# Attention of a graph transformer: where the last unit of a pair is multiplied, and the order of two vector operations in each unit

## The chip, the cores and the metric

One NeuronCore of a Trainium2 chip runs the whole program. The metric is the device time of one execution in microseconds. Engines: PE is TensorE (matmuls; PEld is its weight load), ACT ScalarE, DVE VectorE, POOL GpSimd; SP issues DMAs. Each engine works its own queue in order, and semaphores tie the queues together.

## The reference

Four blocks of a graph network on 3125 nodes with 128 features and 100000 edges, each with a layer norm and a residual. The change touches only the fourth, a transformer of four layers:

```python
for l in range(4):
    Q, K, V = h @ WQ[l] + bQ[l], h @ WK[l] + bK[l], h @ WV[l] + bV[l]
    scores = jnp.sum(Q[dst] * K[src], axis=-1) * scale
    e = jnp.exp(scores - segment_max(scores, dst)[dst])
    attn = e / segment_sum(e, dst)[dst]
    messages = segment_sum(attn[:, None] * V[src], dst)
    h = _layernorm(h + messages @ WO[l] + bO[l], ln_g[l], ln_b[l])
```

## The kernel before

The kernel computes the attention densely. The 3125 nodes are 25 tiles (NT) of 125 (T). A block of 125 destinations gets a row of scores against all 3125 sources; a bias from DRAM, made once from the edge counts, removes the pairs without an edge and gives repeated edges their weight. Blocks go in pairs: pairs 0 to 11 have two blocks ("halves"), pair 12 (LAST_PAIR) has one. `after_pairs` runs pair 0, then a loop over two pairs at a time (their buffers are told apart by e = 1 and 0), then pairs 11 and 12. There are three layers in an outer loop and a fourth written out (its tiles are named l_last_...).

A row of scores is made in 7 chunks (NC), four of 500 and three of 375 columns, so a pair has 14 (PAIR_CHUNKS; g counts them, 0 to 13; g = 14, 15, 16 are chunks 0, 1, 2 of the pair after that). Per chunk:

- **scores** (PE, L1755): three matmuls (high and low parts of q and k), into one of three PSUM banks (S_BANKS). A bank has to have been read: three chunks back, or two back where a new pair begins.
- **maximum** (DVE, L1852): one instruction reads the bank, adds the bias, writes the row buffer and keeps the maximum; a short read of the accumulator follows. After the last chunk of a block, L1858 makes the negated maximum that the exponential needs.
- **exponential** (ACT, L1811): in place on the row buffer. Its schedule, in the step of ACT, is not touched.

The finished rows are turned and multiplied by the values in 13 units (UNITS) of two tiles, the last of one tile. Per unit u:

- **turn** (PE, L1771): four transposes (two in unit 12) into one of three PSUM banks (T_BANKS).
- the **copy** (ACT, L1822): writes the high part of the turned tiles to SBUF (`operand(..., 0)`, tile awcol).
- **low_part** (DVE, L1862): the turned tiles minus their high part.
- **weigh** (PE, L1783): two matmuls per tile, with the high and low parts of the values as weights, which accumulate a pair's sum in `sum_ps[e]`. It waits for low_part of its unit.
- **finish**: ACT (L1817, in unit 1 of the next pair) and DVE (L1870 and L1875, in unit 2) read the sum of the pair before.

The order of the work is written out by hand, in the step function of each engine. On PE a unit of a pair is: scores of chunks ahead, turn(u), weigh(u - 1); after unit 12, weigh(12) stands right behind weigh(11). `ahead` (L1675) says which chunks belong to a unit: AHEAD is 3, so unit 0 takes g = 3 and 4, unit u from 1 on takes g = u + 4, and unit 12 takes g = 16. On DVE a unit is: the maxima of the same chunks, then low_part(u), then in unit 2 the finish. `first` makes the first 17 chunks of a layer before pair 0. Pair 12 makes no scores, and pair 11 has only g = 3 to 6 to make.

Of the kernel before, what the change touches and what calls it, by code (L numbers as in the profile page):

```python
# [25 lines left out]
NC = (NT + 3) // 4  # L26
# [1414 lines left out]
def transformer(nc, G):  # L1441
# [5 lines left out]
    UNITS, PAIR_CHUNKS, HALF, AHEAD = (NT + 1) // 2, 2 * NC, 256, 3  # L1447
    LAST_PAIR = NT // 2
# [3 lines left out]
    with ExitStack() as ctx:  # L1452
# [101 lines left out]
        def layer(l, last, tag):  # L1554
            with ExitStack() as held:
# [20 lines left out]
                with ExitStack() as pre:  # L1576
# [4 lines left out]
                    with nc.Block() as block:  # L1581
                        @block.sync
                        def _(sp):
                            for p in range(2):
                                sp.dma_start(bias[p][:, :], G["bias_dram"][p, :, :]).then_inc(bias_in[p], 16)
# [51 lines left out]
                with ExitStack() as loop:  # L1637
# [21 lines left out]
                    def after_pairs(eng, step):  # L1659

                        step(0, 0)
                        with eng.Fori(0, (LAST_PAIR - 2) // 2) as i:
                            step(2 * i + 1, 1)
                            step(2 * i + 2, 0)
                        step(LAST_PAIR - 1, 1)
                        step(LAST_PAIR, 0)

                    single = lambda P: isinstance(P, int) and P == LAST_PAIR
                    units = lambda P: range(NC if single(P) else UNITS)
# [4 lines left out]

                    def ahead(P, e, u, act_on):  # L1675

                        for k in ((0, 1) if u == 0 else (u + 1,)):
                            g = k + AHEAD
                            to, f = (P + 1, 1 - e) if g < PAIR_CHUNKS else (P + 2, e)
                            half, c = divmod(g % PAIR_CHUNKS, NC)  # L1680
                            if exists(to, half):
                                act_on(to, f, half, c)

                    def first(act_on, chunks=PAIR_CHUNKS + AHEAD):
                        for g in range(chunks):
                            P, (half, c) = g // PAIR_CHUNKS, divmod(g % PAIR_CHUNKS, NC)
                            act_on(P, P, half, c)

                    def operand(P, e, u, low):

                        n, wide = len(tiles(P, u)), T if single(P) else 2 * T
                        buffer = wcol[slot(P, e, u)][:, :, :]
                        if single(P):
                            buffer = buffer.rearrange("p t (a d) -> p (t a) d", a=2)
                        at = low * buffer.shape[2] // 2
                        return buffer[:, 0:n, at:at + wide]

                    def turned(P, e, u):
                        n, wide = len(tiles(P, u)), T if single(P) else 2 * T
                        return turned_ps[slot(P, e, u)][:, 0:n * wide].rearrange("p (t d) -> p t d", d=wide)  # L1700

                    with nc.Block() as block:
# [37 lines left out]
                        @block.tensor  # L1740
                        def _(pe):
                            pe.sem_inc(turned_ready, 2 * UNITS)

                            def scores(P, e, half, c):
                                a, z = CHUNKS[c]
                                b, g = 2 * P + half, NC * half + c
                                if c == 0:
                                    pe.wait_ge(q_staged, 2 * b + 2)

                                back = 3 if g >= S_BANKS else PAIR_CHUNKS + g - max(k for k in range(PAIR_CHUNKS) if k % S_BANKS == g)  # L1750
                                pe.wait_ge(scores_read, b * NC + (c - back + 1 + NC))
                                z += (z - a) % 2
                                terms = ((q_high, k_low), (q_low, k_high), (q_high, k_high))
                                for n, (left, right) in enumerate(terms):
                                    last = pe.matmul(s_ps[g % S_BANKS][:, 0:z - a], left[half][:, :], right[:, a:z],  # L1755
                                                     start=(n == 0), stop=(n == len(terms) - 1))
                                last.then_inc(scores_ready, 1)

                            def turn(P, e, u):
                                ts = tiles(P, u)  # L1760
                                halves = 1 if single(P) else 2
                                pe.wait_ge(exp_done, (2 * P + halves - 1) * NC + (chunk_of(ts[-1]) + 1))
                                if u >= T_BANKS:
                                    pe.wait_ge(low_made, P * UNITS + (u - T_BANKS + 1 + UNITS))
                                else:
                                    before = UNITS + u - T_BANKS if e else max(k for k in range(UNITS) if slot(0, 1, k) == u)
                                    pe.wait_ge(low_made, P * UNITS + (before + 1))
                                for j, t in enumerate(ts):
                                    for half in range(halves):
                                        at = (halves * j + half) * T  # L1770
                                        last = pe.transpose(turned_ps[slot(P, e, u)][:, at:at + T], row[2 * e + half][:, t * T:(t + 1) * T], ident[0:T, 0:T])  # L1771
                                last.then_inc(turned_ready, 1)

                            def weigh(P, e, u):
                                if u == 0:
                                    pe.wait_ge(sum_read, P + 1)
                                pe.wait_ge(low_made, P * UNITS + (u + 1 + UNITS))
                                wide = HALF if single(P) else 2 * HALF
                                buffer = wcol[slot(P, e, u)][:, :, :].rearrange("p t d -> p (t d)")
                                for j, t in enumerate(tiles(P, u)):  # L1780
                                    terms = ((vals_high, wide), (vals_low, HALF))
                                    for n, (left, n_cols) in enumerate(terms if t == 0 else terms[::-1]):
                                        last = pe.matmul(sum_ps[e][:, 0:n_cols], left[:, t, :], buffer[:, j * wide:j * wide + n_cols],  # L1783
                                                         start=(t == 0 and n == 0), stop=(t == NT - 1 and n == 1))
                                if u == units(P)[-1]:
                                    last.then_inc(sum_ready, 1)

                            def step(P, e):

                                for u in units(P):  # L1790
                                    if not single(P):
                                        ahead(P, e, u, scores)
                                    turn(P, e, u)
                                    if u:
                                        weigh(P, e, u - 1)
                                weigh(P, e, units(P)[-1])
                            first(scores)
                            after_pairs(pe, step)

                        @block.scalar  # L1800
                        def _(act):
# [36 lines left out]
                        def _(dve):  # L1838
# [21 lines left out]
                            def low_part(P, e, u):  # L1860
                                dve.wait_ge(high_copied, P * UNITS + (u + 1))
                                dve.tensor_tensor(operand(P, e, u, 1), turned(P, e, u), operand(P, e, u, 0).bitcast(FP32), ALU.subtract  # L1862
                                                  ).then_inc(low_made, 1)
# [12 lines left out]

                            def step(P, e):
                                for u in units(P):
                                    if not single(P):
                                        ahead(P, e, u, maximum)  # L1880
                                    low_part(P, e, u)
                                    if u == 2 and not (isinstance(P, int) and P == 0):
                                        finish(P - 1, 1 - e)
                            first(maximum)
                            after_pairs(dve, step)
                            finish(LAST_PAIR, 0)

# [74 lines left out]
        with nc.Fori(0, LAYERS - 1) as l:  # L1962
            layer(l, False, "l3")
        layer(LAYERS - 1, True, "l3_last")

        with ExitStack() as final:
# [90 lines left out]
```

## Time and profile before

| | us |
|---|---|
| median of 3 runs | 3178.64 (3176.86 to 3182.97) |
| the profiled execution, its own time | 3186.86 |
| its span | 3185.1 |
| PE busy | 2573.7 (81%) |
| DVE busy | 2451.7 (77%) |
| ACT busy | 1956.1 (61%) |
| POOL busy | 221.1 (7%) |

The attention loops lie between about 1725 us and 3150 us of the span. Matmuls are pipelined: a matmul's reported duration (0.39 us for 500 columns) is longer than the distance to the next one's start (0.23 us), so distances between starts show PE's real pace, and an idle time shown before a matmul is shorter than the time lost.

### The profile page before, as it was taken

The page shows a single profiled execution, that of the slowest core. Times are in us where ns is not written, and L with a number is a line of the kernel's source. Part 1 is how long each engine was busy: PE and PEld are TensorE (multiplying, and loading weights), DVE is VectorE, ACT ScalarE, POOL GpSimd, SP SyncE. Part 2 cuts the span into 40 slices and gives each one's busy share as a digit, 9 for nine tenths or more (in the row PEclk, how much of TensorE's full clock was granted, in tenths as well). Part 3 has the DMA queues.
Part 4 walks back from the last instruction along what each step waited for, and adds up shares of the span by engine and source line. Part 5 has one row for each costly group of instructions (what it writes and reads, how often), then busy time and mean ns, then how long its engine had stood idle before and what let it go on. Part 6 is the DMA issues. An engine that isn't in the chain of part 4 may idle for free. (4 is left out here: it accounts for less than half of the span.)

```text
span 3185.1 us, 60275 instructions
## 1 busy us (share of the span) xinstructions
PE 2573.7 (81%) x19197; PEld 2090.7 (66%) x19197; DVE 2451.7 (77%) x5292; ACT 1956.1 (61%) x3958; POOL 221.1 (7%) x487
## 2 busy tenths in 40 slices
PE   0788888756378887888846999789996999969997
PEld 0555555446366666666635888668885888858886
DVE  7999999735489998999976777667775777667776
ACT  1666666512278887788844666556674666646664
POOL 3000000000000000000001111011110111011110
PEclk9999999878689998889978999899998999979998
DMA  1233233462342326332303333033321433123331
GB/s 41 85 115 126 89 124 127 164 219 84 96 128 104 120 102 179 116 109 103 122 5 112 142 123 138 27 140 124 141 103 45 143 133 128 63 103 124 138 136 46
DMA packets 87373, 355.45 MB, mean 112 GB/s; under 512 B 47453, under 2 KB 59541, under 8 KB 59796
## 3 DMA queue, kind: packets, MB, share of 16 engines
q1 hardware_dynamic: 87149, 352.59, 31.9%
q8 instruction: 125, 2.05, 0.3%
q14 instruction: 99, 0.81, 0.1%
HBM read 285.86 MB, written 65.67 MB: 110 GB/s over the span
## 5 line engine op out<-in xcount | busy, mean ns | idle before, releaser
L1822 ACT ACTIVATE awcol<-l_aturned 125x500 fp32r<-125x500 f32 (+2 forms) x489 | 279.2, 572 | 290.8 <-PE l_aturned L1771 288.8
L1365 PE MATMUL gturned<-ident,grow 125*125 125x125 f32 x2500 | 410.3, 306 | 29.2 <-ACT grow L1303 29.2
L1862 DVE TENSOR_TENSOR awcol<-l_aturned,awcol 125x500 fp32r<-125x500 f32 (+2 forms) x489 | 321.2, 657 | 109.9 <-ACT awcol L1822 102.1
L1365 PEld LDWEIGHTS gturned<-ident,grow 125*125 125x125 f32 x2500 | 332.8, 204 | 107.5 <-issue 73.0
L1272 DVE SCALAR_TENSOR_TENSOR grow<-line,a_dst 125x3125 f32<-125x3125 f32 x100 | 347.6, 3476 | 40.3 <-DMA line<-lines_dram 24.7
L1783 PE MATMUL l_asum<-awcol,vals_high 125*128 125x512 f32 (+1 forms) x975 | 360.1, 390 | 19.0 <-DVE awcol L1862 19.0
L1303 ACT ACTIVATE grow<-grow,neg 125x3125 f32<-125x3125 f32 x100 | 290.4, 2904 | 122.6 <-DVE neg L1284 122.6
L1281 DVE CUSTOM_DVE_ANT_0 grow<-grow,bias 125x3125 f32<-125x3125 f32 x100 | 341.7, 3417 | 24.4 <-DMA bias<-bias_dram 10.2
L1343 PE MATMUL gparts<-gwcol,h_mem 125*32 125x125 f32 x5000 | 245.1, 290 | 113.9 <-ACT gwcol L1316 113.9
L1783 PE MATMUL l_asum<-awcol,vals_low 125*128 125x256 f32 x975 | 305.0, 322 | 13.5 <-DVE awcol L1862 12.9
L1316 ACT ACTIVATE gwcol<-gturned 125x1000 f32<-125x1000 f32 x300 | 282.0, 1002 | 19.2 <-PE gturned L1365 19.1
L1343 PEld LDWEIGHTS gparts<-gwcol,h_mem 125*32 125x32 f32 x5000 | 133.3, 114 | 170.7 <-ACT gwcol L1316 73.1
L449 DVE TENSOR_SCALAR hot_key<-iota_key,fixed 128x325 bf16<-128x325 f16 x1000 | 242.2, 315 | 0.0
L503 PE MATMUL win<-hot_key,hot_place 128*125 128x325 bf16 x750 | 140.0, 308 | 122.5 <-DVE hot_key L449 103.7
L1755 PE MATMUL l_scores<-k_low,l_q_high 128*125 128x500 f32 (+1 forms) x525 | 201.3, 383 | 27.5 <-POOL l_q_low L1730 19.3
L564 ACT ACTIVATE blk<-win 125x325 f32<-125x325 f32 x250 | 96.9, 445 | 197.6 <-PE win L514 197.6
L503 PEld LDWEIGHTS win<-hot_key,hot_place 128*125 128x125 bf16 x750 | 90.8, 138 | 189.8 <-DVE hot_key L449 86.4
L1783 PEld LDWEIGHTS l_asum<-awcol,vals_high 125*128 125x128 f32 x975 | 184.7, 189 | 43.2 <-DVE awcol L1862 18.8
L1852 DVE CUSTOM_DVE_ANT_0 arow<-l_scores,abias 125x500 f32<-125x500 f32 (+1 forms) x252 | 154.8, 622 | 74.5 <-PE l_scores L1755 56.8
L1783 PEld LDWEIGHTS l_asum<-awcol,vals_low 125*128 125x128 f32 x975 | 184.8, 190 | 31.8 <-DVE awcol L1862 30.0
L1755 PE MATMUL l_scores<-k_high,l_q_low 128*125 128x500 f32 (+1 forms) x525 | 194.0, 369 | 0.0
L1755 PE MATMUL l_scores<-k_high,l_q_high 128*125 128x500 f32 (+1 forms) x525 | 193.9, 369 | 0.0
(346 smaller groups left out, 5769.8 us busy)
## 6 DMA issues: line engine op xcount, KB each, us to landing
abias<-bias_dram SPq DMA_DIRECT2D x100, 1562.5 KB, 6.5
bias<-bias_dram SPq DMA_DIRECT2D x50, 1562.5 KB, 6.6
bias_dram<-lnrow SPq DMA_DIRECT2D x25, 1562.5 KB, 5.2
counts_dram<-pair SPq DMA_DIRECT2D x13, 1562.5 KB, 6.5
pair<-counts_dram SPq DMA_DIRECT2D x13, 1562.5 KB, 16.4
line<-lines_dram SPq DMA_DIRECT2D x8, 1367.2 KB
fixed<-kp SPq DMA_DIRECT2D x250, 4.0 KB, 1.7
agg<-counts_dram SPq DMA_DIRECT2D x2, 1367.2 KB
```

The costliest lines, as they stand in the source:

```text
L449: last = dve.tensor_scalar(hot_key[p][:, i, keys], G["iota_key"][:, keys], fixed[r][:, k, i, 0:1], base, ALU.subtract, ALU.is_equal)
L503: pe.matmul(win[p][:, k, 0:KEYS[k]], hot_place[p][:, k, i, 0:T], hot_key[p][:, i, keys], start=(i == 0), stop=False)
L1272: dve.scalar_tensor_tensor(out=row[n % RING][:, :], in0=line[g][:, 0, :], scalar=a_dst[:, b, k:k + 1], in1=line[g][:, 1, :], op0=ALU.add, ...
L1281: dve.tensor_tensor_reduce(out=here, in0=here, in1=bias[i % 2][0:T, :], scale=1.0, scalar=-3.0e38, op0=ALU.add, op1=ALU.max, accum_out=top ...
L1303: act.activation(row[n % RING][:, :], row[n % RING][:, :], ACT.Exp, bias=neg[:, b, k:k + 1], accum_out=den[:, b, k:k + 1]).then_inc(exp_do ...
L1316: act.activation(wcol[q % RING][:, :].rearrange("p (g n) -> p g n", g=2), bank[q % RING][:, :, 0:C4], ACT.Copy).then_inc(col_copied, 1)
L1343: last = pe.matmul(part_ps[CH * j:CH * (j + 1), at:at + T], vals[:, t, k, :], wcol[q % RING][:, (t - t0) * T:(t - t0 + 1) * T], start=(t < ...
L1365: last = pe.transpose(bank[q % RING][:, j // 4, j % 4 * T:(j % 4 + 1) * T], row[n % RING][:, t * T:(t + 1) * T], ident[0:T, 0:T])
L1755: last = pe.matmul(s_ps[g % S_BANKS][:, 0:z - a], left[half][:, :], right[:, a:z], start=(n == 0), stop=(n == len(terms) - 1))
L1783: last = pe.matmul(sum_ps[e][:, 0:n_cols], left[:, t, :], buffer[:, j * wide:j * wide + n_cols], start=(t == 0 and n == 0), stop=(t == NT ...
L1822: act.activation(operand(P, e, u, 0), turned(P, e, u), ACT.Copy).then_inc(high_copied, 1)
L1862: dve.tensor_tensor(operand(P, e, u, 1), turned(P, e, u), operand(P, e, u, 0).bitcast(FP32), ALU.subtract).then_inc(low_made, 1)
```

## The change

Three edits in the steps of the attention loop.

1. `ahead` moves every chunk from g = 4 to g = 15 one unit later: unit u takes g = u + 3, and unit 12 takes g = 15 and 16. Before, unit 0 had two chunks; now unit 12 has. `ahead` serves PE (scores) and DVE (maximum) alike.
2. On PE, weigh of a pair's unit 12 no longer follows weigh(11) but stands in unit 0 of the next pair, behind turn(0). After pair 12, its own last unit is weighed at the end, as before.
3. On DVE, low_part(u) comes ahead of the maxima of the unit.

```diff
                     def ahead(P, e, u, act_on):
-                        for k in ((0, 1) if u == 0 else (u + 1,)):
+                        for k in ((u, u + 1) if u == UNITS - 1 else (u,)):
                             g = k + AHEAD
...
                                     turn(P, e, u)
                                     if u:
                                         weigh(P, e, u - 1)
-                                weigh(P, e, units(P)[-1])
+                                    elif not (isinstance(P, int) and P == 0):
+                                        weigh(P - 1, 1 - e, UNITS - 1)
                             first(scores)
                             after_pairs(pe, step)
+                            weigh(LAST_PAIR, 0, NC - 1)
...
                                 for u in units(P):
+                                    low_part(P, e, u)
                                     if not single(P):
                                         ahead(P, e, u, maximum)
-                                    low_part(P, e, u)
                                     if u == 2 and not (isinstance(P, int) and P == 0):
                                         finish(P - 1, 1 - e)
```

## Rows read from the trace of the kernel before

**Rows 1.** Windows, one pair: PE, PEld, DVE, ACT, POOL busy, clock, DMA share.
```profile
2306.16:2330.31 24.15, 23.42 (x143) 20.82 (x143) 17.82 (x46) 16.64 (x43) 3.25 (x8) 1.00 0.37 135
```

**Rows 2.** Waits of PE, 1725 to 3185 us: total us, times, longest.
```profile
PE l_asum L1783 <- DVE awcol L1862: 31.8, 86, 1.1
...
PE l_last_asum L1783 <- DVE awcol L1862: 10.2, 28, 1.1
```

**Rows 3.** Timeline of PE, units inside a pair: start us, duration us, engine, line.
```profile
2321.22 0.33 PE L1755 MATMUL l_scores<-k_low,l_q_high 128*125 128x376 f32 x1
...
2321.73 0.27 PE L1771 MATMUL l_aturned<-ident,x 125*125 125x125 f32 x1
...
2325.59 0.37 PE L1783 MATMUL l_asum<-awcol,vals_low 125*128 125x256 f32 x1
...
2326.37 0.39 PE L1755 MATMUL l_scores<-k_low,l_q_high 128*125 128x500 f32 x1
...
2327.05 0.27 PE L1771 MATMUL l_aturned<-ident,x 125*125 125x125 f32 x1
...
2327.41 0.36 PE L1783 MATMUL l_asum<-awcol,vals_low 125*128 125x256 f32 x1
```

**Rows 4.** Timeline of PE, end of the pair: turn(12), weigh(11), weigh(12), next scores.
```profile
2328.89 0.27 PE L1771 MATMUL l_aturned<-ident,x 125*125 125x125 f32 x1
...
2329.05 0.38 PE L1783 MATMUL l_asum<-awcol,vals_low 125*128 125x256 f32 x1
...
2329.62 0.40 PE L1783 MATMUL l_asum<-awcol,vals_high 125*128 125x512 f32 x1
2330.31 0.38 PE L1783 MATMUL l_asum<-awcol,vals_low 125*128 125x256 f32 x1 [0.29 <-DVE awcol L1862]
...
2330.80 0.49 PE L1755 MATMUL l_scores<-k_low,l_q_high 128*125 128x500 f32 x1
```

**Rows 5.** Timeline of PE, start of the next pair: turn(0), turn(1), weigh(0).
```profile
2332.10 0.60 PE L1771 MATMUL l_aturned<-ident,arow 125*125 125x125 f32 x4
...
2333.05 0.60 PE L1771 MATMUL l_aturned<-ident,arow 125*125 125x125 f32 x4
2334.09 0.50 PE L1783 MATMUL l_asum<-awcol,vals_high 125*128 125x512 f32 x1 [0.44 <-DVE awcol L1862]
```

**Rows 6.** Timeline of ACT: the copies of units 12, 0 and 1.
```profile
2329.30 0.38 ACT L1822 ACTIVATE awcol<-l_aturned 125x250 fp32r<-125x250 f32 x1 [0.33 <-PE l_aturned L1771]
...
2332.74 0.59 ACT L1822 ACTIVATE awcol<-l_aturned 125x500 fp32r<-125x500 f32 x1 [2.36 <-PE l_aturned L1771]
...
2333.91 0.58 ACT L1822 ACTIVATE awcol<-l_aturned 125x500 fp32r<-125x500 f32 x1
```

**Rows 7.** Timeline of DVE: low parts (L1862) and maxima (L1852) in one queue.
```profile
2319.68 0.68 DVE L1862 TENSOR_TENSOR awcol<-l_aturned,awcol 125x500 fp32r<-125x500 f32 x1 [0.22 <-ACT awcol L1822]
2320.43 0.55 DVE L1852 CUSTOM_DVE_ANT_0 arow<-l_scores,abias 125x375 f32<-125x375 f32 x1
...
2323.75 0.55 DVE L1852 CUSTOM_DVE_ANT_0 arow<-l_scores,abias 125x375 f32<-125x375 f32 x1
...
2324.66 0.68 DVE L1862 TENSOR_TENSOR awcol<-l_aturned,awcol 125x500 fp32r<-125x500 f32 x1
...
2331.93 0.68 DVE L1852 CUSTOM_DVE_ANT_0 x<-l_scores,abias 125x500 f32<-125x500 f32 x1 [1.68 <-PE l_scores L1755]
...
2333.36 0.68 DVE L1862 TENSOR_TENSOR awcol<-l_aturned,awcol 125x500 fp32r<-125x500 f32 x1 [0.27 <-ACT awcol L1822]
```

**Rows 8.** Timeline of PE, pair 11 without scores, and its end.
```profile
2757.37 0.60 PE L1771 MATMUL l_aturned<-ident,arow 125*125 125x125 f32 x4
2758.22 0.39 PE L1783 MATMUL l_asum<-awcol,vals_low 125*128 125x256 f32 x1 [0.26 <-DVE awcol L1862]
...
2768.33 0.40 PE L1783 MATMUL l_asum<-awcol,vals_high 125*128 125x512 f32 x1
...
2769.15 1.03 PE L1771 MATMUL l_aturned<-ident,x 125*125 125x125 f32 x8
```

## The prediction

> **What bounds the kernel now.** I read the windows of single pairs first, then the waits of PE, then the timelines of PE, ACT and DVE around one pair's end. A pair takes 24.15 us, and in it PE is busy for 23.42 us, DVE for 17.82 and ACT for 16.64, with TensorE's clock at 2.4 GHz throughout (granted 1.00) [rows 1]. So the attention loop is PE's, and the change can only pay by closing holes in PE. The waits say which: before the matmuls of weigh, PE idles for DVE's low part 86 and 28 times, 31.8 + 10.2 = 42.0 us in the four layers [rows 2]. These idle times understate the loss, as ends of matmuls are modelled, so I go by starts.
>
> Inside a pair, from start to start: turn to weigh 0.36 us (2327.05 to 2327.41), a two-tile weigh 0.78, scores of 500 columns 0.68, of 375 columns 0.51 [rows 3]. A unit is thus 1.82 or 1.65 us and has no hole. At the pair's end there are two:
>
> - Hole A, before weigh(12). Its first matmul starts 0.69 us after the last of weigh(11), where 0.23 (a 512-column step, as between score matmuls) is due: 0.46 lost [rows 4].
> - Hole B, before weigh(0). It starts 1.04 us after turn(1), where 0.36 is due: 0.68 lost [rows 5].
>
> Both have one cause, a latency and not a rate. From the start of turn(0) (2332.10) the copy starts 0.64 later [rows 6], the low part starts at 1.26 and ends at 1.94 [rows 7], and weigh(0) starts at 1.99 [rows 5]. PE has to put 1.99 us of other work between turn(u) and weigh(u). In the middle it has 0.36 + 0.78 + 0.68 + 0.36 = 2.18 or, with 375 columns, 2.01, just enough. Between turn(0) and weigh(0) it had 0.44 (four transposes) + 0.51 + 0.36 = 1.31, hence 0.68 short. DVE's order is not what delays weigh(0) there: its low part waited 0.27 us for ACT's copy, not for the maxima [rows 7].
>
> **The change, part by part.** No instruction is added or removed. I lay PE's new order from the start of turn(11) = 0, by the steps above: weigh(10) 0.36, scores g15 1.14, scores g16 1.82, turn(12) 2.50, weigh(11) 2.66 (0.16 behind turn(12) [rows 4]), scores g3 3.45, turn(0) 4.13, weigh(12) 4.49, scores g4 4.98 (one-tile weigh 0.49 [rows 4]), turn(1) 5.49, weigh(0) due at 5.85.
>
> - Hole A. Copy(12) starts 0.41 us behind turn(12) and takes 0.38 [rows 4, 6], so low part 12 can run from about 3.33 to 3.75. Weigh(12) is due at 4.49: 0.74 to spare. The hole closes: -0.46. What covers it is the scores of g3 and turn(0); without the scores it would be there again with some 0 to 0.1.
> - Hole B. Weigh(0) can't start before 4.13 + 1.99 = 6.12, so 0.27 remain; half of the boundaries lie at the loop's jump, which is in the 0.49, the others have a few hundredths less cover, so I take 0.30. Bounds: 0, if the latency shrinks, and 0.68, as now. Value 0.68 - 0.30 = 0.38 gained.
> - The order on DVE. With low part first, DVE does low 12 at 3.33 and the maxima of g15 and g16 from 3.80, each at most 0.68 [rows 7], and is free at 5.16. Low part 0 wants to start at 4.13 + 1.26 = 5.39: 0.23 to spare. With the old order the maximum of g3 would also stand ahead of it and make it late by 0.45. So this edit does not bring a gain of its own; it keeps the first from being eaten. In the middle of a pair low part 6 (2319.68), say, waited 0.22 us for ACT though a maximum stood ahead [rows 7], so it gains nothing there. A low part and a maximum take 0.75 + 0.68 = 1.43 of the 1.65 to 1.82 us.
> - The maxima come up to a unit and a low part later. Scores wait for a bank read three chunks back, two units and more away; two chunks back at a new pair. Tightest is g14 in unit 11 on the maximum of g12 in unit 9: ready at turn(9) + 1.26 + 0.75 + 0.6 = 2.6, wanted at 1.65 + 0.36 + 0.78 = 2.8. Cost 0, bound 0.5 a pair.
> - The exponential of a block waits for the negated maximum, whose last chunk now falls in units 3 and 10 behind the low part. A 375-column maximum and the negation take 0.91 (2323.75 to 2324.66) [rows 7]: done by turn(3) + 1.26 + 0.75 + 0.91 = 2.92. ACT gets there after copy(4), at about 1.82 + 0.64 + 0.5 = 2.96. Level. A copy with an exponential takes ACT 1.17 (2332.74 to 2333.91) [rows 6] in a unit of 1.82, so 0.65 of lateness would be absorbed. Cost 0.
> - The bias DMAs (SP) and the staging of q (POOL) hang on the maxima of a block's first chunk; both are moved by one unit together with their users, so their lead stays. Cost 0, bound of 0.1 a pair either way.
>
> The DVE queue at hole B bears on a rule. Two instructions in one DVE queue, a low part of 0.68 us and a maximum, start 0.75 us apart (2319.68, 2320.43) [rows 7]: 0.07 between them. The Trainium skill, page "VectorE: DVE Perf Modes", section "The DRAIN you can't avoid", says that behind each operation a flush of roughly its duration less 266 ns passes before the next starts; estimated from that, 0.41 us, the two maxima would push low part 0 to about 6.1, and hole B would be 1.0 instead of 0.3. The trace disagrees with it in this place, and my sum goes by the row.
>
> **The sum.** Per boundary between full pairs 0.46 + 0.38 = 0.84 us. A layer has 11 (into pairs 1 to 11): 9.24. Into pair 12, turn(0) no longer waits behind weigh(12): it started 0.82 us after the last matmul of weigh(11), now 0.23: 0.59 [rows 8], and what follows hangs on its latency. In pair 11 the units without scores lose 0.85 - 0.36 = 0.49 in every second one [rows 8]; unit 3 now has scores, half of 0.49, so 0.25. Pair 0 has no weigh before it and keeps its hole: 0. Together 10.1 a layer, 40.3 in four. The profiled execution took 3186.86 us, so it becomes 3146.6. It lies 8.2 us over the median of the runs, 3178.64; taken from that, 3138.
>
> **The rivals.**
>
> 1. DVE is late at the boundary: low part 0 waits behind the two maxima that now stand in unit 12. For: 0.23 us is all it has to spare. Against: the row of 0.75 us. If it comes late so far that hole B stays 0.68, a boundary gains 0.46, a layer 11 x 0.46 + 0.84 = 5.9, the kernel 23.6: 3155. Late by a whole maximum, hole B is 0.98, a boundary gains 0.16, the kernel 10.4: 3168. The page's rule above is one way to this.
> 2. The two-back bank of g14 makes PE wait in unit 11. For: 0.2 us to spare. If the maximum of g12 comes a low part (0.68) later than laid out, PE loses 0.5 a pair, and the kernel gains 4 x (11 x 0.34 + 0.84) = 18: 3160.
> 3. Slower: ACT finds the negated maximum late in units 4 and 11. It decides from the point where this passes the 0.65 us that ACT absorbs by 0.42 each time, as two of these cancel 0.84. Late by a whole unit, it costs 1.82 - 0.65 = 1.17 twice, 2.34 a pair: 11 x (2.34 - 0.84) x 4, less 3, is 63 us more: 3241. For: the last maximum of a block is moved by a unit and a low part. Against: my two times there are level.
> 4. Hole B closes wholly, as the latency falls when DVE is free: 11 x 0.30 x 4 = 13 more: 3125. Against: it was free before (0.27 us of waiting), and the latency was the same 1.99.
> 5. The change leaves PE as it is, the time going into the next wait: 3178.
>
> **How the numbers follow.** The forecast has 0.68 and spans 3131 to 3147 by itself (latency and boundary terms off by a fifth). Rival 1 has 0.12, rival 2 has 0.06, rival 3 has 0.06, rival 4 has 0.05, rival 5 has 0.03. Range 3124 to 3162: it takes in rivals 4, 2 and the near part of 1. What the measurement can tell from no change is 0.2%, 6.4 us. Faster: the forecast, rivals 1, 2 and 4 but for a hundredth, 0.90; same 0.04; slower 0.06.
>
> **What would show it.** In the profile after: no idle before weigh(12), which stands 0.36 us behind turn(0); weigh(0) about 0.66 us behind turn(1) and 1.99 behind turn(0); a pair of 23.3 us with DVE's and ACT's busy times unchanged; the waits of PE for the low part down from 42 us to under 15. Hole B at 0.68 or more, with DVE's low part 0 shown right behind a maximum without waiting for ACT, is rival 1. A wait of scores on the accumulator read is rival 2. Idle ACT before L1811 in the middle of pairs is rival 3. The forecast is wrong if the pair is outside 23.1 to 23.6 us.

## The result and the profile after

| | before | after |
|---|---|---|
| median of the timed runs, us | 3180.8 (3176.86 to 3185.55) | 3145.24 (3135.67 to 3153.96) |
| profiled execution, us | 3186.86 | 3148.54 |
| its span, us | 3185.1 | 3146.7 |
| a pair, mean of the 40 intervals between full pairs, us | 24.18 | 23.17 |
| four attention loops in the trace, us | 1256.4 | 1212.0 |

The ratio of the runs is 0.9887, with a 95% interval of 0.9853 to 0.9921: the kernel became faster, by 35.6 us at the medians. I forecast 3138, with a range of 3124 to 3162. A pair's length is read from the start of low part 12 (the DVE instruction of L1862, after L1864, with 125x250 elements), which occurs once a pair; a loop goes from the first scores of a layer to the end of its last weigh.

One pair in the windows of the kernel after (busy of PE, PEld, DVE, ACT, POOL, then clock and DMA), to be set beside [rows 1]:

```profile
2295.92:2319.10 23.18, 23.10 (x144) 20.82 (x143) 16.88 (x47) 16.74 (x43) 3.18 (x9) 1.00 0.39 138
```

PE is recorded as busy for nearly all of the pair. Its recorded waits for the low part, 42.0 us before [rows 2], are 7.2 (they understate what is left, as the starts below show):

```profile
PE l_asum L1783 <- DVE awcol L1864: 5.8, 18, 0.7
...
PE l_last_asum L1783 <- DVE awcol L1864: 1.4, 4, 0.7
```

The boundary in PE's timeline of the kernel after, from turn(12) to weigh(0). It answers to [rows 4, 5]:

```profile
2318.27 0.27 PE L1771 MATMUL l_aturned<-ident,x 125*125 125x125 f32 x1
...
2318.41 0.37 PE L1783 MATMUL l_asum<-awcol,vals_low 125*128 125x256 f32 x1
...
2318.96 0.39 PE L1783 MATMUL l_asum<-awcol,vals_high 125*128 125x512 f32 x1
2319.19 0.39 PE L1755 MATMUL l_scores<-k_low,l_q_high 128*125 128x500 f32 x1
...
2319.87 0.60 PE L1771 MATMUL l_aturned<-ident,arow 125*125 125x125 f32 x4
2320.23 0.37 PE L1783 MATMUL l_asum<-awcol,vals_low 125*128 125x256 f32 x1
...
2320.66 0.34 PE L1755 MATMUL l_scores<-k_low,l_q_high 128*125 128x376 f32 x1
...
2321.18 0.60 PE L1771 MATMUL l_aturned<-ident,arow 125*125 125x125 f32 x4
2321.86 0.50 PE L1783 MATMUL l_asum<-awcol,vals_high 125*128 125x512 f32 x1
```

Weigh(12) (2320.23) stands 0.36 us behind turn(0), without a hole. Weigh(0) (2321.86) stands 1.99 us behind turn(0), the same latency to the hundredth as before, and 0.68 behind turn(1), where 0.36 is due: 0.32 of hole B is left. DVE's timeline of the same boundary, low part 12, the maxima of g15 and g16, low part 0, the maximum of g3, answers to [rows 7]:

```profile
2319.10 0.42 DVE L1864 TENSOR_TENSOR awcol<-l_aturned,awcol 125x250 fp32r<-125x250 f32 x1 [0.79 <-ACT awcol L1824]
2319.43 0.68 DVE L1854 CUSTOM_DVE_ANT_0 x<-l_scores,abias 125x500 f32<-125x500 f32 x1
...
2320.04 0.68 DVE L1854 CUSTOM_DVE_ANT_0 x<-l_scores,abias 125x500 f32<-125x500 f32 x1
2320.64 0.08 DVE L1854 DVE_READ_ACCUMULATOR2_ANT l_atop<- 125x1 f32 x1
2321.13 0.68 DVE L1864 TENSOR_TENSOR awcol<-l_aturned,awcol 125x500 fp32r<-125x500 f32 x1 [0.41 <-ACT awcol L1824]
2321.72 0.67 DVE L1854 CUSTOM_DVE_ANT_0 x<-l_scores,abias 125x500 f32<-125x500 f32 x1
```

Low part 0 starts 1.26 us behind turn(0) after 0.41 us of waiting for ACT: DVE is not late.

### The profile page after: what moved, and what is told of

Same layout as the page of the kernel before. It is cut to its first block and busy times, and to the rows that moved or that the text cites. A ratio compares the mean times of both kernels' runs of the same rounds, so it can differ in the third digit from the quotient of the medians.

```text
span 3146.7 us, 60275 instructions
## 1 busy us (share of the span) xinstructions
PE 2569.1 (82%) x19197; PEld 2100.1 (67%) x19197; DVE 2409.8 (77%) x5292; ACT 1961.1 (62%) x3958; POOL 220.1 (7%) x487
## 5 line engine op out<-in xcount | busy, mean ns | idle before, releaser
L1864 DVE TENSOR_TENSOR awcol<-l_aturned,awcol 125x500 fp32r<-125x500 f32 (+2 forms) x489 | 321.5, 657 | 239.9 <-ACT awcol L1824 236.4
L1281 DVE CUSTOM_DVE_ANT_0 grow<-grow,bias 125x3125 f32<-125x3125 f32 x100 | 341.6, 3416 | 24.4 <-DMA bias<-bias_dram 10.1
L1864 DVE TENSOR_TENSOR awcol<-l_last_aturned,awcol 125x500 fp32r<-125x500 f32 (+2 forms) x163 | 107.2, 658 | 79.9 <-ACT awcol L1824 78.7
```

Source lines behind the costliest of these rows:

```text
L1281: dve.tensor_tensor_reduce(out=here, in0=here, in1=bias[i % 2][0:T, :], scale=1.0, scalar=-3.0e38, op0=ALU.add, op1=ALU.max, accum_out=top ...
```

## The experiments

Theory A: the holes are the latency from turn to weigh (1.99 us) less the work that PE has in between, and edit 2 brings the whole gain by putting weigh(12) there. Theory B, from my prediction: the DVE order of edit 3 protects that gain. Each kernel goes by the length of its pairs, which repeats to a few hundredths in one trace, better than whole times do. The first four were timed with the kernel before; the others have one time each.

| kernel | edits | pair, us (mean of 40) | time, us |
|---|---|---|---|
| before | none | 24.18 | 3188.23 beside e1 to e4; 3190.7 beside e5 to e8 |
| e6 | 1 | 24.20 | 3178.09 (one) |
| e3 | 3 | 24.31 | 3193.27 |
| e1 | 2 | 23.22 | 3146.42 |
| e2 | 1, 2 | 23.18 | 3139.36 |
| e5 | 2, 3 | 23.46 | 3154.99 (one) |
| after | 1, 2, 3 | 23.17 | 3145.24 |
| e7 | 2, 3, two chunks in unit 1 | 23.11 | 3138.8 (one) |
| e4 | 2, two chunks in unit 1 | 22.85 | 3123.86 |
| e8 | 1, 2, 3, DVE held | 23.81 | 3168.39 (one) |

### e1: weigh(12) moved, nothing else

```diff
-                                weigh(P, e, units(P)[-1])
+                                    elif not (isinstance(P, int) and P == 0):
+                                        weigh(P - 1, 1 - e, UNITS - 1)
...
+                            weigh(LAST_PAIR, 0, NC - 1)
```

> Only edit 2: weigh of a pair's last unit moves behind turn(0) of the next pair; the chunks ahead and DVE's order stay as before. Theory A (the gain is latency cover, and all of it comes from this edit): laid out from turn(11) = 0, weigh(12) starts 0.36 us behind turn(0) without a hole, and weigh(0) is due 1.67 behind turn(0) and ready at 1.99, so 0.32 of hole B remain, as with all three edits. A pair takes 23.2 us (before 24.19, all three edits 23.17), the kernel about 3145. Theory B (my prediction's reading: the other two edits keep DVE's queue from eating the gain): low part 0 is late by 0.45, hole B is 0.75, a pair takes 23.6 and the kernel about 3165.

Measured: ratio to before 0.9878 (0.9848 to 0.9907), a pair 23.22 us. In PE's timeline turn(0), turn(1) and weigh(0) stand so:

```profile
2312.59 0.60 PE L1771 MATMUL l_aturned<-ident,arow 125*125 125x125 f32 x4
...
2313.89 0.60 PE L1771 MATMUL l_aturned<-ident,arow 125*125 125x125 f32 x4
2314.58 0.50 PE L1783 MATMUL l_asum<-awcol,vals_high 125*128 125x512 f32 x1
```

1.99 us from turn(0) to weigh(0), and 0.69 - 0.36 = 0.33 of hole. Of the 1.01 us that the three edits save a pair, this edit alone saves 0.96. Theory A holds, B falls. (The last 0.04 came with edit 1, in e2; no run shows by what.)

### e2: edits 1 and 2, DVE's order as before

```diff
-                        for k in ((0, 1) if u == 0 else (u + 1,)):
+                        for k in ((u, u + 1) if u == UNITS - 1 else (u,)):
...
-                                weigh(P, e, units(P)[-1])
+                                    elif not (isinstance(P, int) and P == 0):
+                                        weigh(P - 1, 1 - e, UNITS - 1)
```

> Edits 1 and 2 without edit 3: DVE still makes the maxima ahead of the low part. Theory A: the maxima start as soon as their scores are there, so the maximum of g3 ends about 5.2 us behind turn(11) and low part 0 starts on time at 5.4; hole B stays 0.32, a pair 23.2, the kernel 3145: the order on DVE is worth nothing. Theory B, as my prediction put it: the maximum of g3 stands ahead of low part 0 and makes it late by 0.45; hole B 0.75, a pair 23.6, the kernel 3165.

Measured: 0.9855 (0.9826 to 0.9884), a pair 23.18 us, that of the three edits. DVE at the boundary, with the maxima of g16 and g3 ahead of the low parts:

```profile
2328.43 0.68 DVE L1854 CUSTOM_DVE_ANT_0 arow<-l_scores,abias 125x500 f32<-125x500 f32 x1
...
2329.04 0.41 DVE L1864 TENSOR_TENSOR awcol<-l_aturned,awcol 125x250 fp32r<-125x250 f32 x1
2330.04 0.68 DVE L1854 CUSTOM_DVE_ANT_0 arow<-l_scores,abias 125x500 f32<-125x500 f32 x1 [0.58 <-PE l_scores L1755]
...
2330.94 0.68 DVE L1864 TENSOR_TENSOR awcol<-l_aturned,awcol 125x500 fp32r<-125x500 f32 x1 [0.22 <-ACT awcol L1824]
```

The maximum of g3 is done early enough, because with the old order the maxima of g15 and g16 had run earlier too; I had pushed them all behind low part 12 and only then put g3 ahead of low part 0. Edit 3 is worth nothing here.

### e3: DVE's order alone

```diff
+                                    low_part(P, e, u)
                                     if not single(P):
                                         ahead(P, e, u, maximum)
-                                    low_part(P, e, u)
```

> Only edit 3: low part ahead of the maxima on DVE. Hole B is set by the latency turn, copy, low part, and low part 0 waited for ACT before too, so it stays 0.68. Hole A: low part 12 was queued behind the maximum of g16 and ended 0.12 later than it could; it gets 0.12 shorter. Theory A: a pair 24.08 instead of 24.19, the kernel 5 us faster. Rival (the order is a part of the gain of its own): a pair below 23.9, the kernel over 13 us faster. Other rival (low first delays the maxima so that the exponentials or the banks stall): a pair above 24.2.

Measured: 1.0017 (1.0000 to 1.0034), a pair 24.31 us against 24.18. Hole A shrank as expected, from 0.46 to 0.34: the last matmul of weigh(11) and the first of weigh(12) are now 0.57 apart.

```profile
2309.12 0.40 PE L1783 MATMUL l_asum<-awcol,vals_high 125*128 125x512 f32 x1
2309.69 0.39 PE L1783 MATMUL l_asum<-awcol,vals_low 125*128 125x256 f32 x1 [0.17 <-DVE awcol L1862]
```

But the pair got longer, above the 24.2 of the other rival, though not by that rival's mechanism: the waits of PE's scores for a bank and of ACT's exponentials for the negated maximum stay those of the first 20 us of each layer, as before. A new hole opened before weigh(3) instead, which neither I nor a rival had laid out. DVE's queue in units 2 and 3 of this kernel:

```profile
2315.91 0.68 DVE L1862 TENSOR_TENSOR awcol<-l_aturned,awcol 125x500 fp32r<-125x500 f32 x1 [0.53 <-ACT awcol L1822]
2316.51 0.54 DVE L1852 CUSTOM_DVE_ANT_0 arow<-l_scores,abias 125x375 f32<-125x375 f32 x1
...
2317.20 0.16 DVE L1858 TENSOR_REDUCE l_aneg<-l_atop 125x1 f32<-125x7 f32 x1
2317.44 0.41 DVE L1870 TENSOR_REDUCE den<-l_expsum 125x7 f32 x2
2317.83 0.42 DVE L1875 TENSOR_TENSOR cols<-cols,l_asum 128x250 f32 x1
2318.16 0.67 DVE L1862 TENSOR_TENSOR awcol<-l_aturned,awcol 125x500 fp32r<-125x500 f32 x1
```

The maximum of g6, the negation and the finish all stand between low part 2 and low part 3, which starts 2.25 us behind the former without waiting for ACT (PE's turns are 1.84 apart there), and weigh(3) follows turn(4) by 0.57 instead of 0.36:

```profile
2318.32 0.27 PE L1771 MATMUL l_aturned<-ident,x 125*125 125x125 f32 x1
...
2318.89 0.38 PE L1783 MATMUL l_asum<-awcol,vals_low 125*128 125x256 f32 x1
```

So 0.12 was won and 0.21 lost, which is 0.09 of the 0.13 us by which the pair is longer.

### e5: edits 2 and 3, without edit 1

The edits of e1 and e3 together.

> Edits 2 and 3 without edit 1: unit 0 still has two chunks, DVE makes the low part first. From the trace of edit 3 alone: DVE's queue in unit 2 then holds the maximum of g6, the negation and the finish between low part 2 and low part 3, and weigh(3) started 0.21 us late. Theory A (edit 1 matters only because it puts g6 a unit behind the finish): hole A 0, hole B 0.32, and 0.2 before weigh(3): a pair takes 23.4 us, 0.2 more than with edit 2 alone (23.21) and than with all three (23.17). Rival (edit 1 does nothing): 23.2.

Measured: a pair 23.46 us, 0.24 more than e1 and 0.29 more than all three edits. Turn(4) and weigh(3) in PE's timeline:

```profile
2324.18 0.60 PE L1771 MATMUL l_aturned<-ident,arow 125*125 125x125 f32 x4
2324.76 0.39 PE L1783 MATMUL l_asum<-awcol,vals_low 125*128 125x256 f32 x1
```

0.58 instead of 0.36; in the kernel after, with edit 1 added, the distance is 0.36 again. So edit 1 has one clear use in the change: it moves g6 and its negation to unit 3, away from the finish in unit 2, and so takes away edit 3's harm.

### e6: edit 1 alone

The first two lines of e2's diff.

> Only edit 1: unit 12 has two chunks, unit 0 one; weigh(12) still right behind weigh(11), DVE makes the maxima first. Theory A: the work between turn(12) and weigh(12) and between turn(0) and weigh(0) is what it was, so holes A and B stay; low part 12 now stands behind two maxima and is 0.1 later, hole A 0.55. A pair takes 24.2 to 24.3 us (before 24.19). Rival (the distribution of the chunks carries a part of the gain): below 24.0.

Measured: a pair 24.20 us, no change beyond 0.02. Hole A is 0.74 - 0.23 = 0.51, a little larger, as expected (0.55):

```profile
2346.12 0.39 PE L1783 MATMUL l_asum<-awcol,vals_high 125*128 125x512 f32 x1
2346.86 0.39 PE L1783 MATMUL l_asum<-awcol,vals_low 125*128 125x256 f32 x1 [0.34 <-DVE awcol L1862]
```

The one time, 3178.09 beside a single 3190.7 of before, is not a gain of this edit: the four loops of its trace take 1257.3 us, those of before 1256.4.

### e4: two chunks in unit 1 instead of unit 0 or 12

```diff
-                        for k in ((0, 1) if u == 0 else (u + 1,)):
+                        for k in ((0,) if u == 0 else (1, 2) if u == 1 else (u + 1,)):
```

with edit 2, and DVE's order as before.

> Edit 2, DVE's order as before, and another distribution of the chunks ahead: unit 0 takes g3, unit 1 takes g4 and g5, unit u from 2 on takes g = u + 4. Between turn(0) and weigh(0) PE then has 0.36 + 0.43 (weigh 12) + 0.51 + 0.51 + 0.36 = 2.17 us of work, more than the latency of 1.99. Theory A (holes are latency minus work in between): hole B goes to 0, a pair takes 22.85 to 22.9 us instead of 23.17, the kernel about 14 us less than with the three edits, 3131. Rival (the rest of hole B is DVE's or ACT's backlog, or returns at the next unit): a pair at 23.1 or more, the kernel at 3140 to 3150.

Measured: 0.9803 (0.9774 to 0.9832), 3123.86 us, a pair 22.85, as theory A had it (the kernel was expected at 3131). The interval lies below that of the three edits. The windows of one pair, and turn(0), turn(1), weigh(0) in PE's timeline:

```profile
2303.22:2326.04 22.82, 22.82 (x143) 20.78 (x142) 17.85 (x47) 16.73 (x43) 3.16 (x8) 1.00 0.39 144
```

```profile
2326.75 0.27 PE L1771 MATMUL l_aturned<-ident,x 125*125 125x125 f32 x1
...
2328.55 0.27 PE L1771 MATMUL l_aturned<-ident,x 125*125 125x125 f32 x1
...
2328.91 0.48 PE L1783 MATMUL l_asum<-awcol,vals_high 125*128 125x512 f32 x1
```

PE is busy for all of the pair. Weigh(0) follows turn(0) by 2.16 us, which is now PE's own work and above the latency, and turn(1) by 0.36: hole B is closed. This is the best version of the study. It is 21 us below the changed kernel at the medians, which come from different sessions; the four loops of the two traces, 1196.6 and 1212.0 us, differ by 15.4.

### e7: the same with the low part first

e4 with e3's edit.

> As e4 (edit 2, two chunks in unit 1), but with DVE's low part first. Theory A: hole B 0 as there, but in unit 2 the low part, the maximum of g6, the negation and the finish take 0.75 + 0.91 + 0.46 = 2.1 us where 1.8 are there, low part 3 is 0.3 to 0.45 late and weigh(3) 0.2 to 0.3: a pair takes 23.05 to 23.15 us against 22.85. Rival (low part first is harmless or better where the latency counts): 22.85 or less.

Measured: a pair 23.11 us. Edit 3 costs 0.26 us a pair here, again where g6 shares unit 2 with the finish. Weigh(3) follows turn(4) by 0.59 on average, in e4 by 0.36. One such place:

```profile
2294.02 0.27 PE L1771 MATMUL l_aturned<-ident,x 125*125 125x125 f32 x1
...
2294.63 0.39 PE L1783 MATMUL l_asum<-awcol,vals_low 125*128 125x256 f32 x1
```

### e8: DVE held in unit 12

```diff
+                    extra = lsb(f"{tag}_extra", [T, 1])
...
                                         ahead(P, e, u, maximum)
+                                        if u == UNITS - 1:
+                                            dve.tensor_reduce(extra[:, :], vals_low[:, 0:8, :].bitcast(FP32), AX.XY, ALU.max)
```

> All three edits, and once a pair, behind the maximum of g16 in unit 12, DVE makes a reduction over 1024 columns that nothing uses, D about 1.1 us. In the profile after, DVE stood free for 0.41 us before low part 0. Theory A (the queue's margin there is 0.41, and behind it every further microsecond goes to PE): hole B grows by D - 0.41, about 0.7, to 1.0, a pair takes 23.9 us. Rival 1 of the prediction is priced by this: what a late DVE costs at the boundary. Rival (PE has other cover there, DVE's queue doesn't matter): a pair stays at 23.2.

Measured: a pair 23.81 us. DVE's timeline, and PE's turn(0), turn(1), weigh(0):

```profile
2321.89 1.21 DVE L1886 TENSOR_REDUCE l_extra<-vals_low 125x1 f32<-125x1024 f32 x1
2323.02 0.67 DVE L1865 TENSOR_TENSOR awcol<-l_aturned,awcol 125x500 fp32r<-125x500 f32 x1
```

```profile
2321.12 0.60 PE L1772 MATMUL l_aturned<-ident,arow 125*125 125x125 f32 x4
...
2322.43 0.60 PE L1772 MATMUL l_aturned<-ident,arow 125*125 125x125 f32 x4
2323.74 0.50 PE L1784 MATMUL l_asum<-awcol,vals_high 125*128 125x512 f32 x1 [0.71 <-DVE awcol L1865]
```

The reduction holds the queue for 1.13 us (2321.89 to 2323.02). Low part 0 could have started at 2321.12 + 1.26 = 2322.38 and is 0.64 late; weigh(0) is 1.31 behind turn(1), so hole B is 0.95, 0.63 more than 0.32, and a pair is longer by as much. What passes DVE's margin goes to PE one for one. The margin was 1.13 - 0.64 = 0.49 us, where I had expected 0.41 here and laid out 0.23 in the prediction. The prediction took each maximum at its full 0.68 and 0.47 from the low part to the first; the kernel after has low part 12, the maxima and the end of the second 0.33 + 0.61 + 0.60 apart (2319.10, 2319.43, 2320.04, 2320.64).

## Why the prediction was right

- **The bound.** Latency, not DVE's rate: shown. Turn(0) to weigh(0) is 1.99 us before, after and in e1, and grows only where DVE is held (e8) or PE has more work of its own in between (e4, e7).
- **Hole A closes.** Shown in the profile after and in e1, where weigh(12) also follows turn(0) by 0.36; nothing of the other edits is needed.
- **Hole B.** Predicted 0.30 left, measured 0.32.
- **The boundary term was too small:** 0.84 us predicted, 1.01 measured. The holes themselves are right: 0.46 + 0.68 - 0.32 = 0.82. The rest is in what stood around them. A turn followed by scores took 0.44 (turn(0) before), followed by a weigh 0.36: 0.08. Weigh(12) took 0.45 or 0.49, of which only 0.43 are left (2320.23 to 2320.66). And at the loop's jump the scores of g3 and g4 took 1.30 (2330.80 to 2332.10) [rows 4, 5] instead of 0.68 + 0.51: 0.11 at every second boundary, which is gone too. That makes about 0.93 at one boundary and 1.07 at the next; the pairs got 0.97 and, with the jump, 1.09 shorter.
- **The layer.** 10.1 us predicted; in three of the four layers the loop got 12.0, 12.4 and 11.7 shorter (for example 314.35 to 302.37). Ten intervals of 1.01 make 10.1 of it, where the sum had 8.4. The interval into pair 11's end holds the eleventh boundary and the pair without scores; it had 0.84 + 0.25 = 1.09 in the sum and gave 0.82 (20.29 to 19.47). So the 0.25 for pair 11 did not come, and no experiment asked why. The tail with pair 12 had 0.59 and gave 0.53 (12.17 to 11.64); the rest is at the start, which varies by more than that.
- **Why not 48 us then.** One layer gained only 8.3: its pair 0 with the first chunks, which the change hardly touches, took 42.34 us where another's took 39.56, at a granted clock of 0.85 instead of 0.94. The windows of the two starts in the kernel after:

```profile
1734.68:1774.24 39.56, 36.25 (x191) 30.93 (x192) 25.21 (x75) 22.02 (x59) 7.55 (x20) 0.94 0.37 130
2091.38:2133.72 42.34, 39.48 (x191) 34.17 (x192) 25.37 (x75) 22.14 (x59) 7.55 (x20) 0.85 0.35 121
```

  And this execution reached the first attention loop at 1734.68 us, the one before at 1727.49 and the eight of the experiments at 1719 to 1729 (e8, which has all three edits, at 1726.78): 7 us that the change has no part in. 44.4 gained in the loops, about 6 lost elsewhere, makes the 38.3 between the profiled executions. I forecast 40.3. A boundary taken too small and losses that the forecast didn't allow for cancelled in part, and that is luck. Whole times tend to move with the granted clock of the execution: 13 runs of the kernel before, timed beside e1 to e4, go from 3179.01 us at 0.920 to 3196.72 at 0.914, and the four of the kernel after from 3135.67 at 0.920 to 3153.96 at 0.912.
- **Edit 3 was misjudged.** I wrote that it "keeps the first from being eaten". Wrong: e1 and e2 have the gain without it; e3, e5 and e7 show that it costs 0.1 to 0.3 us a pair where the last maximum of a block shares unit 2 with the finish. I had weighed the low part's wait at the boundary and in plain units, and not at the unit whose DVE work is largest.
- **Edit 1** had no gain of its own in the prediction, only risks, and rightly so: alone it changes nothing (e6), on top of edit 2 it is worth 0.04 (e1, e2). What it does, and the prediction did not see, is to make edit 3 harmless. Hole A closes without it (e1).
- **The rivals.** 1: e8 prices it, and a margin of 0.49 us kept it away. 2: the waits of scores for a bank are those at the start of each layer, as before. 3: ACT finds the negated maximum in time (it waits for it once a layer, at the start, as before). 4: hole B didn't close by itself. 5: the pairs did get shorter.
- **Busy times.** I expected DVE's unchanged. It fell from 17.82 to 16.88 a pair with the same instructions, and is 17.84 again in e1 and e2: an artefact of spans that overlap, below.
- **The rule of the Trainium skill** ("VectorE: DVE Perf Modes", "The DRAIN you can't avoid"), as I used it, would have made hole B 1.0 us. That did not come: in the profile after, low part 12 and the two maxima start 0.33 and 0.61 us apart with durations of 0.42 and 0.68. The same section adds that a next operation that is not held starts earlier; my estimate left this out, and these starts agree with it. The row of 0.75 us that I set against the rule [rows 7] did not measure the spacing of the queue: that maximum followed its scores, whose last matmul started at 2319.91.

## What to carry to other kernels

Where three engines hand a tile round, measure the latency from the first instruction to the one that uses the result, and lay out how much work the first engine has between the two at every place of the loop, above all at its seams: the hole is the difference, and moving one piece of work into the gap closes it without making anything faster. Put the surplus work (here the second chunk) into the gap that lacks it, not where the schedule happens to have it. Before an order is changed in all units alike, lay out the unit with the most in its queue; a change of three edits is best timed with each edit alone.

## What the runs showed of the hardware

- Instructions in DVE's queue that wait for nothing overlap in the records: behind a low part of 0.42 the maximum starts 0.33 later, behind one of 0.68, 0.59 later (2321.13, 2321.72), while a maximum of the kernel before, which followed its scores, started 0.75 later [rows 7]. Busy time counts the overlap once, so DVE's busy time fell by 0.9 us a pair without less work (17.82 to 16.88; 17.84 in e1 and e2, which keep the old order).
- The loop's jump is seen in the pairs only where PE had just stalled ahead of it. From low part 12 to low part 12, the intervals with the jump and those inside the loop's body are 24.25 and 24.14 us on average in the kernel before, 24.38 and 24.27 in e3, 24.30 and 24.14 in e6, all with hole A just ahead of the jump. With weigh(12) moved those with the jump are no longer than the others: 23.16 and 23.18 in the kernel after, 23.19 and 23.24 in e1, 23.43 and 23.50 in e5. That a PE with work queued hides the jump is my reading; no run took the jump away.
- The granted clock in the first 40 us of a layer differs between layers of one execution, and the time to the first low part 12 tends to go with it, for example 42.34 us at 0.85, 41.58 at 0.88 (e1, last layer), 39.56 at 0.94, 38.71 at 0.95 (e7, third layer). What decides it was not tested.
